# LayerNorm statistics placed behind each addition, normalisation moved from VectorE to ScalarE, in a four-layer transformer kernel

## What is computed

```python
def _layernorm(x, axis=-1, eps=1e-05):
    m = jnp.mean(x, axis=axis, keepdims=True)
    v = jnp.var(x, axis=axis, keepdims=True)
    return (x - m) / jnp.sqrt(v + eps)

h = _layernorm(x, axis=-1) * (1 + ca) + sa
x = x + ga * attention(h)
h = _layernorm(x, axis=-1) * (1 + cb) + sb
x = x + gb * feed_forward(h)
```

## Time and profile before

| | |
|---|---|
| runs of the kernel | 3218.24, 3220.64, 3225.94 us; median 3220.64 |
| the profiled execution | 3225.6 us, its span 3223.5 us |
| mean granted PE clock | 0.915 of full speed |
| busy, of the span | PE 89%, DVE 72%, ACT 61%, POOL 38% |

### The profile page before, as it was taken

One profiled execution on the slowest core, in us unless ns is written; L12 is line 12 of the kernel. 1 busy time (PEld: TensorE's weight loads), 2 busy tenths in 40 slices (PEclk: granted clock), 3 DMA queues, 4 the chain that ended last, 5 costly groups with the idle time before them and its releaser, 6 DMA issues.

```text
span 3223.5 us, 87828 instructions
## 1 busy us (share of the span) xinstructions
PE 2859.0 (89%) x36283; PEld 1721.4 (53%) x36340; DVE 2318.6 (72%) x3904; ACT 1977.2 (61%) x5621; POOL 1217.3 (38%) x853
## 2 busy tenths in 40 slices
PE   4769869477889799999689999999999999999997
PEld 3634557352244333333256666666666666666664
DVE  4840276449940677777589888888888888888885
ACT  4522365136421266666378887888778887888775
POOL 0010000100100111111167766766776676676662
PEclk7579855688999799999889999999999999999999
DMA  2000000000000200000222233222332332322222
GB/s 105 3 1 0 38 2 4 1 1 0 0 1 0 64 24 24 23 22 21 94 67 66 67 79 99 66 73 65 97 79 68 100 79 68 99 64 61 61 68 52
DMA packets 48238, 153.38 MB, mean 48 GB/s; under 512 B 11553, under 2 KB 13857, under 8 KB 45953
## 3 DMA queue, kind: packets, MB, share of 16 engines
q1 hardware_dynamic: 47872, 148.17, 17.5%
HBM read 43.60 MB, written 5.44 MB: 15 GB/s over the span
## 4 chain that ended last, share of the span: by engine, by line
PE 71%; DVE 15%; ACT 7%; issue 3%; DVEq 2%; DMA 1%; POOLq 1%; ACTq 1%; POOL 0%; SPq 0%
PE ps L1549 13%; PE ps L673 7%; PE ps L1567 5%; PE ps L1602 5%; DVE arena L1040 4%; PE ps L1144 4%; PE ps L1172 4%; PE ps L1611 4%; PE ps L1624 4%; PE ps L1159 3%; PE ps L1584 3%; PE ps L1593 2%; PE ps L1630 2%; PE ps L308 2%; DVE arena L2017 1%
## 5 line engine op out<-in xcount | busy, mean ns | idle before, releaser
L1549 PE MATMUL ps<-arena 128*128 128x512 f32 x1152 | 563.6, 612 | 16.4 <-ACTq L1836 15.9
L1901 ACT ACTIVATE arena<-ps,arena 128x64 f32<-128x64 f32 x1536 | 458.8, 318 | 85.8 <-DVE arena L2097 82.0
L2174 POOL TENSOR_TENSOR arena<-arena 128x1024 f32<-128x1024 f32 x190 | 447.4, 2360 | 98.0 <-DVE arena L1986 98.0
L2180 POOL TENSOR_TENSOR arena<-arena 128x2048 f32<-128x2048 f32 x95 | 344.3, 3624 | 225.2 <-ACT arena L1843 220.3
L1309 DVE TENSOR_REDUCE arena<-ps 128x1 f32<-128x512 f32 x512 | 329.3, 686 | 77.5 <-PE ps L1144 72.4
L1271 ACT ACTIVATE arena<-ps 128x1024 f32<-128x1024 f32 x256 | 262.2, 1024 | 178.8 <-PE ps L1159 170.1
L1901 ACT ACTIVATION_READ_ACCUMULATOR arena<-ps,arena 128x1 f32 x1536 | 323.5, 211 | 0.0
L1549 PEld LDWEIGHTS ps<-arena 128*128 128x128 f32 x1152 | 197.8, 191 | 181.9 <-issue 157.6
L1981 DVE TENSOR_TENSOR arena<-ps,arena 128x1024 f32<-128x1024 f32 x192 | 234.0, 1219 | 47.2 <-PE ps L1549 32.9
L1986 DVE TENSOR_TENSOR arena<-ps,arena 128x512 f32<-128x512 f32 x384 | 245.2, 680 | 0.0
L2169 POOL TENSOR_TENSOR arena<-arena 128x512 f32<-128x512 f32 x192 | 200.7, 1046 | 88.0 <-DVE arena L2023 87.5
(11 more groups left out here) (291 smaller groups left out, 5530.1 us busy)
## 6 DMA issues: line engine op xcount, KB each, us to landing
arena<-pack_l SPq DMA_DIRECT2D x144, 256.0 KB
arena<-grow SPq DMA_DIRECT2D x144, 256.0 KB
arena<-in_deep SPq DMA_DIRECT2D x6, 2649.5 KB, 10.4
arena<-pack_l SPq DMA_DIRECT2D x96, 128.0 KB
arena<-grow SPq DMA_DIRECT2D x84, 128.0 KB
arena<-in_rotary SPq DMA_DIRECT2D x6, 1024.0 KB, 7.5
...
```

Of the source, the lines that this page charges most:

```text
L1549: last = T.matmul(m.ps[0:rows.stop - rows.start, at + half, :], f.xs[t % 2][:, rows], w.wqkv[:, j * INNER + half * BLK:j * INNER + (half + ...
L1901: last = A(f.prob[:, p, :], m.ps[:, 4 + j % 2, i * SPAN:(i + 1) * SPAN], ACT.Exp, bias=f.nmax[t % 2][:, p:p + 1], accum_out=f.rsum[t % 2][ ...
L2174: G.tensor_tensor(f.rot[t % 2][:, here], f.rot[t % 2][:, here], f.sin[:, here], ALU.add)
L2180: G.tensor_tensor(r, r, spread(f.ss[t % 2], DH), ALU.mult).then_inc(s["rotated"], 1)
```

## The change

Where the diff names new line numbers they are those of the changed kernel.

- `ln_vector` is gone. `ln_block` makes the statistics of one block, and DVE runs it right behind the addition that completes the block: behind each of the four additions of a half, and in the experts behind pieces 2, 3, 5 and 6, which complete blocks 0 to 3. It has one drain more, ahead of `bn_stats`, since x has just been written. Only LayerNorm 0 has no addition in front; its four blocks stand alone.
- POOL makes, besides `rstd`, a `shift` = -mean * rstd for each token: two more instructions of 128 x 4 and a drain for each block.
- The 16 normalising instructions are now on ACT: `activation` with Identity, scale `rstd` and bias `shift`, one value of each per partition. ACT normalises block g + 1 before it writes `hT` of block g.
- The meetings between a half and the LayerNorm behind it are gone; PE and ACT go from their part of the half straight to their part of the LayerNorm. The meeting behind each LayerNorm stays. 10 meetings are left of 17.
- PE turns the tiles into banks 4 to 7 where `LN_BANKS` says 4 and into banks 0 to 3 otherwise.
- SP waits for 4, 8, 9 and 10 stages instead of 5, 14, 16 and 17. The last three are the same places of the program as before; the reload of the ternary weights comes one LayerNorm later (behind LayerNorm 2).

```diff
@@ -168,20 +168,16 @@
 
 
-def ln_vector(nc, dve, m, s, k):
-    for g in range(NBLK):
-        tiles = range(4 * g, 4 * g + 4)
-        for t in tiles:
-            nc.vector.bn_stats(m.stats[:, t, :], m.x[:, t, :])
-        dve.drain()
-        for t in tiles:
-            last = nc.vector.bn_aggr(m.mv[:, t, :], m.stats[:, t, :])
-        last.then_inc(s["stats"], 1)
-    for t in range(TILES):
-        if t % 4 == 0:
-            dve.wait_ge(s["rstd"], NBLK * k + t // 4 + 1)
-        nc.vector.tensor_scalar(m.xn[:, t, :], m.x[:, t, :], m.mv[:, t, 0:1], m.rstd[:, t:t + 1],
-                                ALU.subtract, ALU.mult).then_inc(s["xn"], 1)
+def ln_block(nc, dve, m, s, k, g):
+
+    tiles = range(4 * g, 4 * g + 4)
+    dve.drain()
+    for t in tiles:
+        nc.vector.bn_stats(m.stats[:, t, :], m.x[:, t, :])
+    dve.drain()
+    for t in tiles:
+        last = nc.vector.bn_aggr(m.mv[:, t, :], m.stats[:, t, :])
+    last.then_inc(s["stats"], 1)
 
 def ln_gpsimd(nc, pool, m, s, k):
@@ -190,23 +186,42 @@
         pool.wait_ge(s["stats"], NBLK * k + g + 1)
         nc.gpsimd.tensor_scalar(m.rstd[:, here], m.mv[:, here, 1], EPS, None, ALU.add)
         pool.drain()
-        nc.gpsimd.tensor_tensor(m.rstd[:, here], m.rstd[:, here], m.nhalf[:, 0:4], ALU.pow).then_inc(s["rstd"], 1)
+        nc.gpsimd.tensor_tensor(m.rstd[:, here], m.rstd[:, here], m.nhalf[:, 0:4], ALU.pow)
+        nc.gpsimd.tensor_scalar(m.shift[:, here], m.mv[:, here, 0], -1.0, None, ALU.mult)
+        pool.drain()
+        nc.gpsimd.tensor_tensor(m.shift[:, here], m.shift[:, here], m.rstd[:, here], ALU.mult).then_inc(s["rstd"], 1)
+
+
+
+LN_BANKS = (0, 4, 0, 4, 0, 0, 0, 4)
 
 def ln_tensor(nc, pe, m, s, k):
     for g in range(NBLK):
         pe.wait_ge(s["xn"], TILES * k + 4 * (g + 1))
         for t in range(4):
-            last = nc.tensor.transpose(m.ps[:, g, t * P:(t + 1) * P], m.xn[:, 4 * g + t, :], m.ident)
+            last = nc.tensor.transpose(m.ps[:, LN_BANKS[k] + g, t * P:(t + 1) * P], m.xn[:, 4 * g + t, :], m.ident)
         last.then_inc(s["turned"], 1)
 
 def ln_scalar(nc, act, m, s, k, l, sub):
-    for g in range(NBLK):
+    def normed(g):
+        act.wait_ge(s["rstd"], NBLK * k + g + 1)
+        for t in range(4 * g, 4 * g + 4):
+            nc.scalar.activation(m.xn[:, t, :], m.x[:, t, :], ACT.Identity, bias=m.shift[:, t:t + 1],
+                                 scale=m.rstd[:, t:t + 1]).then_inc(s["xn"], 1)
+
+    def modulated(g):
         b = g // (NBLK // BATCH)
         act.wait_ge(s["turned"], NBLK * k + g + 1)
-        nc.scalar.activation(m.hT[:, g * BLK:(g + 1) * BLK], m.ps[:, g, :], ACT.Identity,
+        nc.scalar.activation(m.hT[:, g * BLK:(g + 1) * BLK], m.ps[:, LN_BANKS[k] + g, :], ACT.Identity,
                              bias=mod_col(m, l, sub, 0, b), scale=mod_col(m, l, sub, 1, b))
+
+    normed(0)
+    for g in range(1, NBLK):
+        normed(g)
+        modulated(g - 1)
+    modulated(NBLK - 1)
 
 MOD_SEMS = ("silu", "cols", "wide", "rows")
...
@@ -581,6 +596,7 @@
         b = i // (NBLK // BATCH)
         add_gated(nc, dve, m, m.ps[:, 4 + i, :].rearrange("p (a b) -> p a b", a=4), 4 * i, 4,
                   repeat(gate_row(m, g.layer, ATTN, b), 4), g.tmp[:, i % 2, :].rearrange("p (a b) -> p a b", a=4))
+        ln_block(nc, dve, m, ln, 2 * g.layer + 1, i)
 
 def gla_gpsimd(nc, pool, m, s, g):
...
@@ -722,6 +738,7 @@
         dve.wait_ge(s["y"], f.done["y"] + i + 1)
         add_gated(nc, dve, m, m.ps[:, i, :].rearrange("p (a b) -> p a b", a=4), 4 * i, 4,
                   repeat(f.row[:, i // 2, :], 4), f.tmp[:, i % 2, :].rearrange("p (a b) -> p a b", a=4))
+        ln_block(nc, dve, m, ln, 2 * f.layer + 2, i)
 
 
...
@@ -880,6 +897,8 @@
         wide = m.ps[:, bank, 0:n * WIDE2].rearrange("p (a b) -> p a b", b=WIDE2)
         add_gated(nc, dve, m, wide[:, :, 0:P], tiles[0], n, repeat(gate_row(m, 1, FFN, bank // 3), n),
                   f.tmp[:, bank % 2, 0:n * P].rearrange("p (a b) -> p a b", a=n))
+        if bank % 3:
+            ln_block(nc, dve, m, ln, 4, 2 * (bank // 3) + bank % 3 - 1)
 
 MOLE_SEMS = ("low", "gated", "turned", "zT", "hid", "hidden", "logits", "exped", "y")
...
@@ -2416,15 +2438,15 @@
             for k in ("l0", "tern", "l1", "mole", "l2", "l3"):
                 sp.dma_start(m.packs[k][:, :], d[k]).then_inc(m.loaded[k], 16)
 
-            sp.wait_ge(m.stage_done, ENGINES * 5)
+            sp.wait_ge(m.stage_done, ENGINES * 4)
             sp.dma_start(m.packs["tern"][:, :], d["tern2"]).then_inc(m.loaded["tern"], 16)
 
-            sp.wait_ge(m.stage_done, ENGINES * 14)
+            sp.wait_ge(m.stage_done, ENGINES * 8)
             mha_sync(nc, sp, m, attn_s[3], attn_m[3])
 
-            sp.wait_ge(m.stage_done, ENGINES * 16)
+            sp.wait_ge(m.stage_done, ENGINES * 9)
             deep_sync(nc, sp, m, ffn_s[3], ffn_m[3])
-            sp.wait_ge(m.stage_done, ENGINES * 17)
+            sp.wait_ge(m.stage_done, ENGINES * 10)
             sp.dma_start(out.rearrange("b (t p) f -> p (b t) f", p=P), m.x[:, :, :]).then_inc(m.out_written, 16)
             sp.wait_ge(m.out_written, 16)
             for name, loaded in m.loaded.items():
@@ -2436,13 +2458,12 @@
             finish_stage(pe, m, 0)
             for l in range(LAYERS):
                 ln_tensor(nc, pe, m, ln, 2 * l)
-                finish_stage(pe, m, 1 + 4 * l)
+                finish_stage(pe, m, 1 + 2 * l)
                 (gla_tensor, gla_tensor, ssm_tensor, mha_tensor)[l](nc, pe, m, attn_s[l], attn_m[l])
-                finish_stage(pe, m, 2 + 4 * l)
                 ln_tensor(nc, pe, m, ln, 2 * l + 1)
-                finish_stage(pe, m, 3 + 4 * l)
+                finish_stage(pe, m, 2 + 2 * l)
                 (tern_tensor, mole_tensor, tern_tensor, deep_tensor)[l](nc, pe, m, ffn_s[l], ffn_m[l])
-                finish_stage(pe, m, 4 + 4 * l)
+            finish_stage(pe, m, 9)
 
         @block.scalar
         def _(act):
...
@@ -2464,15 +2484,14 @@
             dve.wait_ge(m.loaded["x"], 32)
             mod_vector(nc, dve, m, mod)
             finish_stage(dve, m, 0)
+            for g in range(NBLK):
+                ln_block(nc, dve, m, ln, 0, g)
             for l in range(LAYERS):
-                ln_vector(nc, dve, m, ln, 2 * l)
-                finish_stage(dve, m, 1 + 4 * l)
-                (gla_vector, gla_vector, ssm_vector, mha_vector)[l](nc, dve, m, attn_s[l], attn_m[l])
-                finish_stage(dve, m, 2 + 4 * l)
-                ln_vector(nc, dve, m, ln, 2 * l + 1)
-                finish_stage(dve, m, 3 + 4 * l)
-                (tern_vector, mole_vector, tern_vector, deep_vector)[l](nc, dve, m, ffn_s[l], ffn_m[l])
-                finish_stage(dve, m, 4 + 4 * l)
+                finish_stage(dve, m, 1 + 2 * l)
+                (gla_vector, gla_vector, ssm_vector, mha_vector)[l](nc, dve, m, attn_s[l], attn_m[l], ln)
+                finish_stage(dve, m, 2 + 2 * l)
+                (tern_vector, mole_vector, tern_vector, deep_vector)[l](nc, dve, m, ffn_s[l], ffn_m[l], ln)
+            finish_stage(dve, m, 9)
 
         @block.gpsimd
         def _(pool):
@@ -2481,19 +2500,18 @@
             finish_stage(pool, m, 0)
             for l in range(LAYERS):
                 ln_gpsimd(nc, pool, m, ln, 2 * l)
-                finish_stage(pool, m, 1 + 4 * l)
+                finish_stage(pool, m, 1 + 2 * l)
                 if l in (0, 1):
                     gla_gpsimd(nc, pool, m, attn_s[l], attn_m[l])
                 if l == 2:
                     ssm_gpsimd(nc, pool, m, attn_s[l], attn_m[l])
                 if l == 3:
                     mha_gpsimd(nc, pool, m, attn_s[l], attn_m[l])
-                finish_stage(pool, m, 2 + 4 * l)
                 ln_gpsimd(nc, pool, m, ln, 2 * l + 1)
-                finish_stage(pool, m, 3 + 4 * l)
+                finish_stage(pool, m, 2 + 2 * l)
                 if l == 3:
                     deep_gpsimd(nc, pool, m, ffn_s[l], ffn_m[l])
-                finish_stage(pool, m, 4 + 4 * l)
+            finish_stage(pool, m, 9)
```

More of the change, by code:

```diff
@@ L465, in gla_scalar, with gla_vector @@
           scale=g.nw).then_inc(s["oT"], 1)
-def gla_vector(nc, dve, m, s, g):
+def gla_vector(nc, dve, m, s, g, ln):
     V = nc.vector
@@ L707, in tern_scalar, with tern_vector @@
                 n += 1
-def tern_vector(nc, dve, m, s, f):
+def tern_vector(nc, dve, m, s, f, ln):
     n = 0
@@ L835, in mole_scalar, with mole_vector @@
                     .then_inc(s["hidden"], 1)
-def mole_vector(nc, dve, m, s, f):
+def mole_vector(nc, dve, m, s, f, ln):
     V = nc.vector
@@ L1005, in ssm_gpsimd, with ssm_vector @@
     nc.gpsimd.tensor_tensor(y, y, f.xc[:, 0, :], ALU.mult).then_inc(s["gated"], 1)
-def ssm_vector(nc, dve, m, s, f):
+def ssm_vector(nc, dve, m, s, f, ln):
     V = nc.vector
@@ L1055, in ssm_vector @@
                   repeat(gate_row(m, 2, ATTN, i // 2), 4), f.tmp[:, i % 2, :].rearrange("p (a b) -> p a b", a=4))
+        ln_block(nc, dve, m, ln, 5, i)
```

(13 more changed lines are left out.)

## The result

| | before | changed |
|---|---|---|
| median of 18 runs | 3225.22 us (3217.88 to 3227.9) | 3228.52 us (3224.54 to 3230.5) |
| the profiled execution | 3225.6, span 3223.5 | 3225.27, span 3223.5 |
| mean granted PE clock in it | 0.915 | 0.915 |
| busy, of the span | PE 89%, DVE 72%, ACT 61% | PE 89%, DVE 71%, ACT 63% |

The ratio is 1.0016, with an interval of 1.0009 to 1.0023. I had predicted 3218.4 us, a gain of 0.07%, with 3227 as the upper end. The change is within the 0.2% that I held for likeliest, but on the other side of zero, and the interval doesn't take in 1.

The account below looks back on a forecast made before the run. PE, busy 89% of the span, was taken to bound the kernel: -6.1 us without the clock and +3.9 for it net -2.2, from 3225.6 to 3223.4, less 5.0 to the median: 3218.4 us, range 3209 to 3227.

Parts of the forecast that it names:

- the hole of 2.12 us: DVE's idle time between two additions ahead of LayerNorms 2 and 6; the 1.40 us of statistics should fit into it.
- the POOL term: POOL's chain for a block behind the last statistics, pow to multiplication: 2.10 us, with 0.30 for the multiplication.
- the rival of the dear chain: POOL's multiplication takes the pow's 1.04 us: 8.2 us more over all LayerNorms, result 3226.6 us; chance 0.08.
- POOL is the bound: At LayerNorm 0, POOL's blocks of 2.10 us outlast DVE's of about 1.4, so the first matmul comes 2.6 us later.
- the clock term: Thin turns leave PE's clock low at first matmuls: about 1.7 us each behind LayerNorms 0 and 1, 0.5 behind 3; +3.9.
- the first rival: Gaps between PE's turns don't matter to the clock: 3214.5 us, or 3207.7 if it stays up elsewhere too; chance 0.3.
- the second rival: The clock rises late at every stage behind a LayerNorm: 3227 us at d = 6.1, 3233 at 8.2; chance 0.12.
- turning point, d = 4.1: d is the time from a stage's first matmul until the clock is up; from 4.1 us the change gains nothing.

Follow-up runs that it names:

- the cut one: The changed kernel without the deep block of the last layer, 1589.97 us; the kernel before, without it too, took 1584.60 us.
- front_before_warm: The kernel before without the deep block, plus 24 to 26 extra matmuls ahead of each LayerNorm's first turn: 1583.88 us.
- front_ln0: The changed kernel without the deep block, but DVE normalises LayerNorm 0 as before: 1583.72 us.
- front_warm_rest: The changed kernel without the deep block, plus extra matmuls between PE's turns at LayerNorms 0, 2, 4, 5, 6 and 7: 1578.67 us.
- front_warm_1_3: The changed kernel without the deep block, plus extra matmuls between PE's turns at LayerNorms 1 and 3 alone: 1587.69 us.

## Why the prediction was wrong

**What held.** At LayerNorm 2 the statistics fit into the holes of DVE and the additions kept their pace. The timeline of the changed kernel:

```profile
364.47 0.69 DVE L233 TENSOR_TENSOR arena<-ps,arena 128x512 f32<-128x512 f32 x1 [0.72 <-PE ps L698]
365.23 0.69 DVE L235 TENSOR_TENSOR x<-x,arena 128x512 f32<-128x512 f32 x1
365.32 0.70 POOL L190 TENSOR_SCALAR shift<-mv 128x4 f32<-128x4 f32 x1
...
370.52 0.38 DVE L179 BATCH_NORM_AGGREGATE mv<-stats 128x2 f32<-128x6 f32 x4
...
373.08 1.65 ACT L211 ACTIVATE arena<-x,shift,rstd 128x128 f32<-128x128 f32 x4 [0.80 <-POOL shift L192]
...
376.78 8.87 PE L285 MATMUL ps<-hT,pack_l 128*128 128x512 f32 x16 [0.89 <-ACTq L103]
```

Of the hole of 2.12 us, 0.72 is left: 1.40 went to the statistics, as worked out. The tail, from the end of the last `bn_aggr` to the first matmul, was forecast at 5.87 us and is 5.88 at LayerNorm 1 (206.27 to 212.15). Two errors nearly cancel in it: the multiplication on POOL takes 0.20 and not 0.30, and ACT's four instructions take 1.65 and not 1.50, since one follows the other after 0.40, not 0.35. My reason for 0.35 (x lies in SBUF and not in PSUM) had no row behind it, and no run here bears it out. The estimate of 1.64 us from the figures of the Trainium skill, ScalarE: Activation LUTs, What ACT_TABLE_LOAD costs, agrees with the trace. With it the sum would have been 1.1 higher; the POOL term gives most of that back.

The groups by shape, after, settle the rival of the dear chain:

```profile
L211 ACT ACTIVATE arena<-x,shift,rstd 128x128 f32<-128x128 f32 x128 | 52.7, 482 | 107.3 <-POOL shift L192 107.3
...
L189 POOL TENSOR_TENSOR rstd<-rstd,nhalf 128x4 f32<-128x4 f32 x32 | 33.9, 1058 | 4.7 <-issue 0.3
...
L192 POOL TENSOR_TENSOR shift<-shift,rstd 128x4 f32<-128x4 f32 x32 | 6.4, 199 | 4.7
```

At LayerNorm 0 POOL is the bound, as forecast: its blocks follow each other at 2.1 to 2.2 us without a pause, and the first matmul comes 2.8 us later.

```profile
29.80 0.23 POOL L187 TENSOR_SCALAR rstd<-mv 128x4 f32<-128x4 f32 x1 [28.92 <-DVE mv L179]
...
31.97 0.23 POOL L187 TENSOR_SCALAR rstd<-mv 128x4 f32<-128x4 f32 x1
...
38.12 0.20 POOL L192 TENSOR_TENSOR shift<-shift,rstd 128x4 f32<-128x4 f32 x1
...
42.18 8.92 PE L285 MATMUL ps<-hT,pack_l 128*128 128x512 f32 x16 [0.89 <-ACTq L103]
```

The last row is also the direct sight of the clock's price: the same 16 matmuls took 7.13 us before.

One reading in the prediction was wrong and did no harm: the 0.07 us behind a drain stand ahead of the `bn_aggr`, not ahead of the statistics. Measured, the addition at 365.23 is followed by the first statistics 0.77 later, against the 0.76 used.

**The first step that failed** is the size of the clock term, +3.9 us. The mechanism was the right one, the forecast that the clock would never be up at a stage's first matmul came true at every LayerNorm, and the first rival (gaps don't matter) fell. But I let the clock rise after 3.4 us everywhere, as it did behind LayerNorm 2 before, when turns had been dense for 4 us in front of it. Behind sparse turns it took 4.3 us on average. Half of the low time that was added in the two profiles is 4.0 us behind LayerNorms 0 and 1 (forecast: 3.4) and 1.5 behind 2, 4, 5 and 6 (forecast: nothing); the experts, to which I gave 0.5, lost 1.7 in the whole kernel and 1.9 in the cut one. That makes +7.2 instead of +3.9. The formula of the second rival, 3.15 d - 6.8, gives +6.7. Medians give more, 3.3 + 6.1 = 9.4 in the whole kernel and 5.4 + 5.4 = 10.8 in the cut ones; the same account of the two cut profiles is +8.2, so 2 to 3 us are left that no start of a stage explains. So of the rivals the second is the one that happened, at its mild end: its turning point, d = 4.1, was passed by little. I had given it 0.12.

**The second step** is the base. I took 5.0 us off for the distance between the profiled execution and the median of three runs. Over the 18 runs beside the changed kernel the kernel before has 3225.22 us, at the profiled execution's 3225.6; three runs that scatter over 8 us did not carry such a correction. Nor does the profiled execution by itself: beside the three sets of experiments the same kernel had 3218.96, 3222.06 and 3220.11. Of the miss of 10.1 us, 4.6 are this, 5.5 the forecast of -2.2 where +3.3 was measured. Without the 4.6 the measured time would have been inside the range, and the sign wrong all the same.

**What stays open.** Why front_before_warm gained so little, and front_ln0 more than its place explains. What the clock does inside the attentions enters. Attention 0 runs at the low clock for most of its time whatever stands in front of it, and its length goes roughly with how long. Its shortest and its longest case, front_warm_rest and front_warm_1_3, whole stage each:

```profile
42.94:193.58 150.64, 86.89 (x1976) 68.16 (x1977) 93.17 (x194) 81.63 (x210) 5.67 (x2) 0.60 0.01 2
```

```profile
42.08:197.80 155.72, 92.70 (x1976) 72.17 (x1977) 93.34 (x195) 81.75 (x210) 5.67 (x2) 0.55 0.01 2
```

That is 119.5 and 138.6 us at the low clock. In the pair of whole kernels the change had 126.5 where the kernel before had 133.6, and in attention 1 187.9 against 194.3. With that it fits that attentions 0 and 1 came out 0.2 and 1.9 us shorter there, although they started with the clock low for longer, and that the two profiles show only +2.8 in the stages. What sets these totals, and the falls near the end of the deep block, no run here shows.
